# Last feed-forward of a four-block network: one root for two norms, silu through tanh, the final batch tile by tile

## The reference, cut to what matters

```python
def rms_norm(x):     return x * rsqrt(mean(x * x) + EPS)          # EPS = 1e-5
def act_quant(x):    s = 127 / clip(max|x|, 1e-5); return clip(round(x * s), -128, 127) / s
def bitlinear158(x, w, b):  return act_quant(rms_norm(x)) @ ternary(w).T + b
def layer_norm(x, g, b):    return (x - mu) * rsqrt(var + EPS) * g + b
h = silu(bitlinear158(x, w1, b1))             # 256 -> 1024
h = gelu(h, approximate=False)
h = layer_norm(h, ln_g, ln_b)
y = bitlinear158(h, w2, b2)                   # 1024 -> 256
# outside: x = x + tanh(g_ffn[1]) * y(_layernorm(x)), _layernorm with the same EPS
```

## Time and profile before

| what | value |
|---|---|
| median of 3 runs | 614.12 us |
| span of the profiled execution, first to last instruction | 612.1 us |
| what lies around the span, by the median | about 2.0 us |
| PE busy | 495.7 us (81%) |
| DVE busy | 478.0 us (78%) |
| ACT busy | 349.4 us (57%) |
| POOL busy | 280.9 us (46%) |
| slots of the attention | about 305 to 575.3 us |
| feed-forward of batch 3, alone | 575.3 to 612.1 us |

### The profile page before, as it was taken

How to read it: one execution, slowest core, us unless ns; L and a number is a source line. 1 busy time by engine, 2 the same in 40 slices (tenths; PEclk the granted TensorE clock), 3 DMA queues, 4 the chain that set the end, 5 groups by cost and what they waited for, 6 DMA issues and landing times.

```text
span 612.1 us, 10074 instructions
## 1 busy us (share of the span) xinstructions
PE 495.7 (81%) x3003; PEld 367.9 (60%) x3003; DVE 478.0 (78%) x1298; ACT 349.4 (57%) x785; POOL 280.9 (46%) x264
## 2 busy tenths in 40 slices
PE   6917777878699389999879999998799988997723
PEld 3302222323288257676679899987689878995602
DVE  4899999999859557987446765895899869756865
ACT  2775554545158132221347666679665996798453
POOL 4129777788010454550048638832776233323211
PEclk9958999979889599999969999999899999999866
DMA  6929100000015399994232103300223000000000
GB/s 165 224 69 376 24 1 0 1 34 1 9 35 176 88 269 299 287 291 140 77 138 70 36 2 70 62 9 2 36 51 70 1 2 1 19 1 1 2 17 17
DMA packets 43816, 48.60 MB, mean 79 GB/s; under 512 B 5644, under 2 KB 40054, under 8 KB 43510
## 3 DMA queue, kind: packets, MB, share of 16 engines
q1 hardware_dynamic: 39926, 36.46, 20.7%
q0 software_dynamic: 3840, 11.54, 8.0%
HBM read 41.43 MB, written 6.56 MB: 78 GB/s over the span
## 4 chain that ended last, share of the span: by engine, by line
PE 33%; DVE 24%; issue 21%; ACT 11%; POOL 8%; DMA 3%; DVEq 1%; SPq 0%; POOLq 0%; ACTq 0%
DVE hst L1670 7%; PE ps L1426 5%; PE ps L1369 4%; PE ps L1370 4%; PE ps L1371 4%; PE ps L1415 3%; DVE hc L1679 2%; DMA G<-token_rows,idx_x 2%; POOL dbu L501 2%; PE ps L1289 2%; ACT pr L860 2%; PE ps L1326 2%; POOL G L580 1%; POOL G L558 1%; DVE ebuf L1806 1%
## 5 line engine op out<-in xcount | busy, mean ns | idle before, releaser
L596 POOL TENSOR_TENSOR pn<-pr,pinv 128x512 f32<-128x512 f32 x64 | 67.6, 1058 | 92.8 <-DVE pinv L2029 92.2
L501 POOL TENSOR_TENSOR dbu<-du,brow 128x512 f32<-128x512 f32 x64 | 81.4, 1282 | 42.0 <-DVE du L1663 23.2
L1122 PE MATMUL ps<-hc,ident 128*128 128x512 f32 x128 | 76.6, 690 | 27.6 <-DVE hc L1679 26.0
L1670 DVE TENSOR_TENSOR_SCAN hst<-ps,dbu 128x512 f32<-128x512 f32 x64 | 77.5, 1211 | 0.2 <-POOL dbu L501 0.2
L722 ACT ACTIVATE ps<-dtv,amat 128x510 f32<-128x510 f32 x64 | 44.1, 690 | 49.2 <-DVE hst L1670 48.3
L860 ACT ACTIVATE pr<-ebuf,smin 128x256 f32<-128x256 f32 x128 | 63.7, 502 | 12.1 <-DVE smin L2020 6.2
L1426 PE MATMUL ps<-pT,cS 128*128 128x256 f32 x256 | 67.4, 386 | 0.0
L558 POOL DMA_INDIRECT G<-token_rows,idx_x x32 | 39.9, 1246 | 57.7 <-DVE wkv L1815 28.5
L1122 PEld LDWEIGHTS ps<-hc,ident 128*128 128x128 f32 x128 | 21.9, 206 | 67.1 <-DVE hc L1679 63.2
L580 POOL DMA_INDIRECT G<-expert_out,idx_g x48 | 51.7, 1078 | 11.6 <-issue 10.2
L1369 PE MATMUL ps<-xnT,mqk 128*128 128x256 f32 x128 | 47.8, 374 | 6.9 <-DVE qT L1995 4.1
(11 more groups left out here) (346 smaller groups left out, 1374.9 us busy)
## 6 DMA issues: line engine op xcount, KB each, us to landing
wdn<-in_L_ffn_wd SPq DMA_DIRECT2D x15, 384.0 KB, 10.3
wgu<-in_L_ffn_wg SPq DMA_DIRECT2D x14, 384.0 KB, 6.3
wgu<-in_L_ffn_wu SPq DMA_DIRECT2D x14, 384.0 KB, 8.5
expert_out<-xn SPq DMA_DIRECT2D x16, 256.0 KB, 4.5
wq<-in_L_xattn_Wq SPq DMA_DIRECT2D x1, 2048.0 KB, 9.3
wo<-in_L_xattn_Wo SPq DMA_DIRECT2D x1, 2048.0 KB, 15.1
wo<-in_L_ffn_w SPq DMA_DIRECT2D x2, 1024.0 KB, 7.4
x<-in_x SPq DMA_DIRECT2D x1, 1024.0 KB, 6.7
```

Of the source, the lines that this page charges most:

```text
L501: nc.gpsimd.tensor_tensor(dbu[:, j, :], du[:, j % 2, 512 * hb:512 * hb + 512], brow[:, j // 2, :], ALU.mult).then_inc(pool_dbu, 1)
L596: nc.gpsimd.tensor_tensor(pn[:, h % 2], pr[:, h % 2], pinv[:, h % 2, :].unsqueeze(2).to_broadcast([P, 2, L]), ALU.mult)\
L1122: pe.matmul(bank(2 + j % 2), ident[:], hc[:, j % 2, :], start=(isinstance(m, int) and m + k == 0), stop=(isinstance(m, int) and m + k == N ...
L1670: V.tensor_tensor_scan(hst[:, j, :], bank(j % 2), dbu[:, j, :], 0.0, ALU.mult, ALU.add)\
```

## The change

1. **One root.** The front's layer norm and RMS norm have one factor: with variance v, rsqrt(v + e) * rsqrt(v/(v + e) + e) = rsqrt(v(1 + e) + e^2). DVE only subtracts the mean and finds the largest at once; POOL takes one root in place of two; the factor enters with the rounding scale.
2. **silu through tanh.** ACT computes tanh(h/2) into `tanhs`; DVE then forms (tanh + 1) * h, which is 2 silu(h), in place (`gated`); gelu reads it with scale 0.5. `preload` at slot 64 takes Gelu, not Silu. `sneg` moves in `ebuf` to make room.
3. **Second bias early.** `b2v` is multiplied by the gate once; POOL adds it to the rows of x (`rest_rows`); the gate goes into `fback`; `finish` is then one operation per tile, not two and a common one.
4. **Tile by tile.** After the loop, tile 0 runs ahead of tile 1 on every engine, the last attention output is added per tile (`tail_add`), both tiles take their layer norm from ACT's sums, the last copies of tile 1 are made by DVE in place of ACT, and `finish(2)` moves back behind `tail_gated(0, 1)`.
5. Four semaphores of the scan stage are merged into others, with the same order of waits.

```diff
+            def root_front(f):
+                pool.wait_ge(f_var[0], f + 1)
+                nc.gpsimd.tensor_tensor(frt[:, 0, :], fve[:, 0, :], mhalf[:, 0:2], ALU.pow).then_inc(f_root[0], 1)
+            def rest_rows(f):
+                pool.wait_ge(f_gated, 2 * f + 1)
+                rows = x[:, 2 * f:2 * f + 2, :]
+                nc.gpsimd.tensor_tensor(rows, rows, b2v.unsqueeze(1).to_broadcast([P, 2, H]), ALU.add)\
+                    .then_inc(f_rest, 1)
...
                     if at == 5:
-                        root_of(f, 0, 0)
-                    if at == (6 if f < B - 2 else 5):
-                        root_of(f, 0, 1)
+                        root_front(f)
+                    if at == (14 if f < B - 2 else 12):
+                        rest_rows(f)
...
             def silu(f, k):
                 act.wait_ge(f_h, 2 * f + k + 1)
-                A(hbuf[:, k, :], hbuf[:, k, :], ACT.Silu).then_inc(f_silu, 1)
+                wait_count(act, f_act, 6 * f)
+                A(tanhs[k], hbuf[:, k, :], ACT.Tanh, scale=0.5).then_inc(f_silu, 1)
             def gelu(f, k):
-                act.wait_ge(f_silu, 2 * f + k + 1)
-                A(hbuf[:, k, :], hbuf[:, k, :], ACT.Gelu, accum_out=fsum[:, k:k + 1]).then_inc(f_act, 1)
+                act.wait_ge(f_gated, 2 * f + k + 1)
+                A(hbuf[:, k, :], hbuf[:, k, :], ACT.Gelu, scale=0.5, accum_out=fsum[:, k:k + 1]).then_inc(f_act, 1)
...
+            def gated(f, k):          # DVE: k = 1 at 13 (11 for f = 2), ahead of o_low; k = 0 at 12 (10), behind q_low
+                dve.wait_ge(f_silu, 2 * f + k + 1)
+                V.scalar_tensor_tensor(hbuf[:, k, :], tanhs[k], 1.0, hbuf[:, k, :], ALU.add, ALU.mult)\
+                    .then_inc(f_gated, 1)
...
             def finish(f):
...
                 for k in range(2):
-                    last = V.scalar_tensor_tensor(yb[:, k, :], ps[:, 7, H * k:H * k + H], fback[:, 1, k:k + 1], b2v,
-                                                  ALU.mult, ALU.add)
-                last.then_inc(f_end, 1)
-                dve.wait_ge(f_end, f + 1)
-                V.scalar_tensor_tensor(yb, yb, tg[:, 3:4], x[:, 2 * f:2 * f + 2, :], ALU.mult, ALU.add)\
-                    .then_inc(f_out, 1)
+                    last = V.scalar_tensor_tensor(yb[:, k, :], ps[:, 7, H * k:H * k + H], fback[:, 1, k:k + 1],
+                                                  x[:, 2 * f + k, :], ALU.mult, ALU.add)
+                last.then_inc(f_out, 1)
...
 # ACT, after the loop
             tail_turned(0)
+            tail_tanh(0, 0)
+            tail_tanh(0, 1)
             tail_turned(1)
-            tail_silu(0, 0)
-            tail_silu(0, 1)
-            tail_silu(1, 0)
-            tail_silu(1, 1)
             tail_gelu(0, 0)
             tail_gelu(0, 1)
-            tail_gelu_whole()
-            tail_deviation()
+            tail_deviation(0)
+            tail_tanh(1, 0)
+            tail_tanh(1, 1)
+            tail_gelu(1, 0)
+            tail_gelu(1, 1)
+            tail_deviation(1)
             tail_squares(0)
             tail_squares(1)
...
 # DVE, after the loop (new order)
+            tail_add(0); tail_stats(0); tail_norm(0); tail_add(1); tail_round(0); tail_stats(1); tail_norm(1)
+            tail_hidden(0, 0); tail_hidden(0, 1); tail_round(1); tail_gated(0, 0); tail_gated(0, 1); finish(B - 2)
+            tail_hidden(1, 0); tail_hidden(1, 1); tail_middle(0); tail_centred(0); tail_gated(1, 0); tail_gated(1, 1)
+            tail_variance(0); tail_normal(0); tail_middle(1); tail_centred(1); tail_variance(1); tail_largest(0)
+            tail_mean_square(0); tail_normal(1); tail_largest(1); tail_mean_square(1)
...
+            tail_whole(0); tail_whole(1); tail_backs(); tail_turned_hidden(0); tail_turned_hidden(1)
             tail_finish(0)
             tail_finish(1)
```

More of the change, by code:

```diff
@@ L260, in build_program @@
         squared = flat_a[:, 5 * FI:6 * FI]
+        tanhs = (squared, ebuf[:, 4 * H:8 * H])
+        middles = (ebuf[:, 0:4 * H], tanhs[1])
         xf = xn[:, 4:6, :]
@@ L655, in _ @@
                         root_of(f, 1, 1)
[L656 to L659, removed]
+            tail_root_front(0)
+            tail_root_front(1)
+            rest_rows(B - 1)
             tail_root(1, 0, 0)
@@ L916, in tail_turned, with tail_tanh @@
                 A(xqT[:, H * k:H * k + H], bank(k).bitcast(BF16)[:, 0:H], ACT.Copy).then_inc(f_qT, 1)
-            def tail_silu(k, n):
+            def tail_tanh(k, n):
                 act.wait_ge(f_h, 2 * B - 2 + 2 * k + n + 1)
-                part = hbuf[:, k, 512 * n:512 * n + 512]
[L922 to L938, removed]
+                act.wait_ge(f_act, 6 * B - 6)
+                A(tanhs[k][:, 512 * n:512 * n + 512], hbuf[:, k, 512 * n:512 * n + 512], ACT.Tanh, scale=0.5)\
+                    .then_inc(f_silu, 1)
@@ new lines, in tail_gelu, with tail_deviation @@
+            def tail_gelu(k, n):
+                act.wait_ge(f_gated, 2 * B - 2 + 2 * k + n + 1)
+                part = hbuf[:, k, 512 * n:512 * n + 512]
+                A(part, part, ACT.Gelu, scale=0.5, accum_out=fhalf[:, k, n:n + 1]).then_inc(f_act, 1)
+            def tail_deviation(k):
+                act.wait_ge(f_mean, B + k)
+                act.wait_ge(f_act, 6 * B - 6 + 3 * k + 2)
+                A(squared, hbuf[:, k, :], ACT.Square, bias=fmean[:, k:k + 1], accum_out=fdev[:, k:k + 1])\
+                    .then_inc(f_act, 1)
@@ L1002, in _ @@
                 if slot == NH * B:
-                    preload(1, ACT.Silu)
+                    preload(1, ACT.Gelu)
                 if b + 1 < B:
@@ L2054, in steps_of, with back_scaled @@
                 return step, sync
+            def back_scaled(step, w, some):
+                if w:
+                    step(V.tensor_scalar(fback[:, 1, some], famax[:, 1, some], wmean[:, 1:2], tg[:, 3:4],
+                                         ALU.mult, ALU.mult))
+                else:
+                    step(V.tensor_scalar(fback[:, 0, some], famax[:, 0, some], wmean[:, 0:1], None, ALU.mult))
             def scales(step, sync, w):
-                step(V.tensor_tensor(famax[:, w, :], famax[:, w, :], frm[:, w, :], ALU.mult))
+                root = (frt[:, 0, :], frm[:, 1, :])[w]
+                step(V.tensor_tensor(famax[:, w, :], famax[:, w, :], root, ALU.mult))
                 sync()
@@ L2285, in tail_centred @@
+                dve.wait_ge(p_exp, NH * B)
+                step(V.scalar_tensor_tensor(middles[k], hbuf[:, k, :], fmean[:, k:k + 1], lng, ALU.add, ALU.mult))
                 tail_at["c", k] = tail_step[1]
@@ L2342, in _ @@
                 more = b + 1 < B
-                if h == 5 and 0 < b <= B:
+                if h == 5 and 0 < b < B:
                     add_attention(b - 1)
@@ L2369, in _ @@
                         hidden(f, 0)
+                    if at == 13 and f < B - 2:
+                        gated(f, 1)
+                    if at == 11 and f == B - 2:
+                        gated(f, 1)
                     if at == 15 and f == B - 2:
@@ L2408, in _ @@
                         front_stats(f)
+                    if at == 5 and f == 0:
+                        dve.wait_ge(d_kv, 32 + 64)
+                        V.tensor_scalar(b2v, b2v, tg[:, 3:4], None, ALU.mult)
                     if at == 7:
                         front_round(f)
+                    if at == (12 if f < B - 2 else 10):
+                        gated(f, 0)
                     if at == 10 and f < B - 2:
```

246 lines of the change are left out of this document (127 added, 119 removed).

## The result

The changed kernel took 610.45 us (median of 6 runs, 606.94 to 612.51) beside 614.84 us for the kernel before (6 runs): ratio 0.9913 [0.9884, 0.9942]. A second measurement gave 608.7 us beside 614.98: 0.9913 [0.9879, 0.9946]. That is 5.3 us off 614.84, between 3.6 and 7.1; the forecast was 6.8.

What follows compares the result with a forecast made beforehand. No engine was full beside feed-forwards, PE waiting some 4 us; PE bound heads alone, and after 575.3 us all was a chain. Slots 4.3 plus tail 2.5 gave 6.8 us, 614.1 to 607.3 us; range 603.5 to 612.5.

Steps and rivals of the forecast that it cites:

- Slots: Loop's feed-forward slots: removed table loads and new gates together gain 1.6 + 1.6 + 1.1 = 4.3 us over three batches.
- this copy would start when PE's transposes are done, about 486.3: Batch 1, ACT's copy of the next batch's rows: without the silu loads, gelu's load and what follows come 1.5 us earlier.
- PE's wait for ACT's copy: Slots of batches 0 and 1: PE's 1.9 us wait for the copy of the transposed probabilities goes.
- The wait for the next batch's rows: Slots of batches 0 and 1: PE's wait grows from 0.6 to 1.0 us.
- Batch 2: Last feed-forward in the slots: gelu can start 1.1 us sooner, nothing being prepared for a next batch.
- Front, `finish`, `rest_rows`, bias: Small DVE and POOL steps in the loop: worth nothing; cost or gain under 1.1 us in all.
- Tail: After the loop: 1.5 us to tile 0's scale, 0.4 and 0.5 later, 0.1 from PE's clock, 2.5 us gained.
- The first milestone: Tail, attention's last sum to tile 0's rounded rows: 3.8 us instead of 7.4, 3.6 us earlier, not kept.
- The old tail's load at 1.28 us: Tail, ACT at 589.37: table load between silu and gelu, in the chain; none left after the change.
- Rivals 2 and 4: 2: gelu's table lacks tanh, tail loads, 608.6 us, chance 0.12. 4: exponential's table lacks it, near 613.9 us, 0.03.
- Rival 3: Slots: DVE becomes the bound, all six gates on PE's path, 7.7 us, loads worth nothing; 619.3 us, chance 0.05.
- Rival 1: Slots: gelu starts no earlier, waiting for DVE's `gated` in slot 13; slots lose 0.8 us, 612.4 us, chance 0.17.

Runs made afterwards that it cites:

- gates later: Changed kernel with batches 0 and 1's first gate moved behind the mask, the second behind the low parts: ratio 0.9867 [0.982, 0.9915].
- small gates: Changed kernel with `gated` in the slots working on 2 of 1024 columns: ratio 0.9906 [0.9883, 0.993].
- the loads out: Kernel before with tanh in place of silu in the slots, six table loads fewer and no gate added: ratio 0.9953 [0.9928, 0.9978].

## Why the prediction was right, and where it was wrong

The sign and the size hold: 607.3 us forecast, 610.45 and 608.7 measured, within the range; 5.3 us gained of 6.8. But two terms missed in opposite directions, the slots by 2.4 us and the tail by 1.5, and that the total comes out near is in part luck.

- **Slots: 4.3 us forecast, 1.9 found** (173.9 to 172.0): the loads brought 3.2, the front and the other small steps 0.9, and the gates took 2.2. The step that failed is "this copy would start when PE's transposes are done, about 486.3". With the silu pair gone ACT did catch up, and then waited 0.91 us for DVE's mask, because I took DVE's order as it stood and forgot that the first gate (slot 12) is ahead of the mask of slot 13. I counted the gates only on the path of DVE's low parts, not on that of ACT's exponentials, behind which copy and load stand. Gelu's load came at 485.83, 2.6 us earlier by the clock but only some 0.3 us against PE's own progress, where I had 1.5. From the start of head 20's transposition to that of head 36, batch 0 gained 0.6 us and from there to head 52, batch 1, 0.2 us, against 1.6 each. Of the gates' 2.2 us, 1.7 come from their place (gates later: 170.2 us of heads; small gates: 169.8).
- The same step assumed that PE's wait for ACT's copy would go. It fell from 1.9 to 1.1 us, and stayed at 1.9 with the loads out and no gates: gelu's load and both gelus stand ahead of that copy, whatever happens before them. With the loads out gelu's load does come 1.1 us sooner after PE's transposes in batch 1, near the 1.5 forecast, and PE is then sooner too.
- **The wait for the next batch's rows**, forecast at 1.0 us, is 1.2: right, and for the reason given, the gate ahead of the low parts.
- **Batch 2: 1.1 us forecast**, 40.38 to 39.28 us from head 52 to head 62, 1.1. Right: nothing is prepared there for a next batch, and with the gates small it takes 39.31, so they cost nothing there.
- **Front, `finish`, `rest_rows`, bias: nothing forecast, 0.9 us gained** (169.8 against 170.7 us), within the 1.1 that I gave as a bound. "DVE and POOL do that beside a busy PE; I put it at nothing" is the step that was wrong: in the kernel before PE waits for DVE's low part of the queries in batch 0 (0.35 us behind head 26 with the loads out), and not in the changed one.
- **Tail: 2.5 us forecast, about 4.0 found.** The first milestone is exact (3.8 us). The mis-sized term is the root, which I left at the 1.57 us of the earlier trace rows: in the new order no DVE operation with two wide inputs runs beside the two variance roots, and they take 0.55. That took 1.0 us from the way to tile 0's second product, and about 0.6 more up to the scale, which came 3.1 us earlier instead of 1.5; how much of those 0.6 is the second root's was not measured apart. As an estimate from the rows, a root of 1.57 us from 590.91 on would have held back the product at 592.00 by 0.5 us. From the scale to the end the gain was 0.9 us (36.79 - 32.80 - 3.1), as forecast (0.4 + 0.5), in two profiles whose last products both took 1.03 us.
- **The old tail's load at 1.28 us, wholly on the chain**: shown, by the old tail without it (1.3 us, 1.4 in its middle) and by DVE's wait (1.4 us).
- **The start of the attention's last sum, about 571.0**: 571.70, but 1.2 us of the fall come from the stage before the loop, so this agreement proves less than it seems.

Rivals 2 and 4 fell with the count of loads. Rival 3 fell: six gates on DVE cost 2.2 us, not 7.7. Rival 1 said that gelu would start no earlier because DVE holds it back. For batches 0 and 1 it was nearly right, though by a wait that it did not name (the mask, not the gate of slot 13): with the gates where they are the loads bring 0.3 us there, and 1.1 in batch 2. It was wrong that the slots would lose.

The rule by which the prediction lets a DVE operation with two SBUF inputs and a POOL one exclude each other was used for the danger and not for the gain. I priced it for the new gates, where five of six took 1.21 to 1.22 us and one, in batch 2 beside POOL's division, 1.58:

```profile
541.48 1.58 DVE L2150 SCALAR_TENSOR_TENSOR wgu<-ebuf,wgu 128x1024 f32<-128x1024 f32 x1
```

I didn't ask which POOL operations of the old tail had been paying for it.

## What to carry to other kernels

When work leaves an engine, follow that engine to its next instruction and look what that one waits for: the gain ends at the first wait, and here a new operation on the other engine had been put in front of exactly that. Before calling an added operation free or dear, try its place: the same six operations cost 2.2 us with four of them ahead of the mask and the low parts, and 0.5 us with these four behind them. Before reading a difference of two profiles, look where the same code already differs: counted in, the step of 0.8 us at head 22 would make the small gates look as if the front brought nothing. A duration that a row shows holds for that row's neighbours; if the change moves the neighbours, bound it by the shortest row of its kind.

## What the runs showed of the hardware

- The same work ahead of the loop ended between 301.7 and 307.3 us. A single run of this kernel can't show a change of under 5 us; a stretch cut on PE's own marks shows 0.2 us, once the two steps that scatter are left out.
